# Four-layer block kernel: twenty turns written out in place of a loop of two, and a new order of the pieces on four engines

## Chip, cores and metric

The kernel runs on one core of a Trainium2 chip. The metric is the device time of one execution in microseconds (us), the median of several runs; less is better. The profile comes from one more execution.

## What is computed

Input x is 32 sequences of 256 tokens with 128 features, in fp32. Four layers follow one another, and each is `x = layernorm(x + layer(x))`, the norm over the features and without weights:

```python
q, k = rope(x @ Wq.T), rope(x @ Wk.T)         # 8 heads of 16
v, gate = x @ Wv.T, x @ Wg.T
num = (q @ (k.T @ v)) * scale + v.sum(tokens)
den = (q @ k.sum(tokens)) * scale + 256
layer1 = ((num / den + conv5(v)) * gate) @ Wo.T
layer2 = x @ W.T + lw[top1] * (x @ Wd[top1].T) @ Wu[top1].T   # ranks 1, 2, 4, 8
layer3 = softmax(mask(q @ k.T / sqrt(128))) @ v               # causal, one head
layer4 = sum(w[e] * swiglu_e(x) for 4 of 16 experts) + swiglu_shared(x)
```

In layer 2, `lw` is the softmax of four scaled cosine similarities and top1 its largest entry. In layer 4 a sigmoid router picks two of four groups of experts and then four experts; the sixteen experts have 64 hidden features each, the shared one 128.

## The kernel before, in words

**Blocks and turns.** The 8192 tokens are cut in 16 blocks of 512 (two sequences, four tiles of 128 tokens). A block goes through the kernel in five turns. Turn i works on layer 1 of block i (pieces whose names begin with `a_`), layer 2 and the projections of layer 3 of block i-1 (`b_`, `c_xT`, `c_project`, `c_value`), the attention of layer 3 and the router of block i-2 (`c_`, `r_`), the experts of block i-3 (`d_`), and the output of block i-4 (`d_yT`, `d_res`, `e_norm`). There are 20 turns. Turns 0 to 2 lack later layers, turns 16 to 19 earlier ones; turns 3 to 15 have all of `a`, `b`, `c` and `d`, and are called full here. The engines share no barrier: each runs its own list of pieces in order, and a piece begins with waits on semaphores that count what the others have finished. So the order of the pieces in the function `turn` of each engine sets the order of the work, and a piece whose input is late holds up all that stands behind it on its engine.

**Loop.** Each engine writes out turns 0 to 5 (`LEAD = 6`), then runs a hardware loop of two turns five times (turns 6 to 15), and then has turns 16 to 19 written out again. Two turns stand in a turn of the loop since some buffers alternate.

**Pieces on TensorE.** `a_xT_` transposes x (L378), `a_vT_` makes v transposed (L384), `a_qk` q and k (L390), `a_g_` the gate (L402), `a_v_` transposes the centred v back (L415), `a_kv` multiplies k and v (L406), `a_qT_` transposes q (L420), `a_num_` makes numerator and denominator (L424), `a_aT` transposes the result (L432), `a_out` applies Wo (L436). `b_small` (L449) makes all small projections of layer 2, `b_dnT` and `b_up` the low-rank part (L457, L461). `c_scores`, `c_pT`, `c_av` (L486, L500, L507) are layer 3's attention. `r_xT`, `r_gate` (L516, L520) feed the router, `d_cT` (L526) transposes the expert weights. The experts come in nine chunks of 128 hidden features, eight routed and one shared: `d_hidden(c)` (L532) writes gate and up products of chunk c into the banks GB and UB, in three products of split fp32r operands each, and `d_down(c)` (L548) adds the chunk's output in bank YB. d_hidden(c) waits for silu and for gu of chunk c-1, which empty GB and UB.

**ScalarE** evacuates most banks (`x0_hi`, `a_vT_`, `a_g_`, `a_v_`, `a_qT_`, `copy_xT`, `b_small`, `b_dnT`, `c_pT`, `c_qkv`, `r_hi`, `d_y`), takes exponentials (`c_exp`, `b_exp`, `r_exp`) and silu (`d_silu(c)`, L734), applies norms (`c_norm`, `b_layer_norm`, `e_norm`) and the first tap of the convolution (`a_tap0`, L676). Exponential and silu need different tables; a table load of 1.28 us stands before the first of either kind after the other.

**VectorE** multiplies silu by the up product (`d_gu(c)`, L1063) and that by the transposed expert weight (`d_hid(c)`, L1072), does rope (`a_rope`, L836), masks the k-v product into kv_m (`a_kv`, L845), adds the other four taps (`conv_tap`, L947), takes reciprocals of the denominator (`a_den`, L855), divides (`a_att`, L862), adds convolution and mean (`a_mix`), and takes row maxima (`c_max`), residual sums (`a_res`, `c_res`, `d_res`) and statistics of every norm (`norm_stats`, `b_res`, L1001). The router's small operations are `b_norm`, `b_logits`, `b_first`, `b_weigh` for layer 2 and `r_groups(0..4)`, `r_combine` for layer 4.

**GpSimd** subtracts the high parts (`x0_lo`, `x3_lo`), adds the two halves of rope (`a_rope`, semaphore g_qk), gates (`a_gate`) and turns statistics into scale and shift (`ln_of(k)`, one per norm). `split_late` splits the experts' weights into high and low parts once, in turn 1, on ScalarE (L629) and VectorE (L816). SP issues loads and stores (L309 on).

Of the kernel before, what the change touches and what calls it, by code (L numbers as in the profile page):

```python
# [111 lines left out]
def build(nc, x_dram, weight_dram, whole_dram, out_dram):  # L112
    blocks = x_dram.shape[0] // BLOCK
    LEAD = 6
    loops = (blocks - LEAD) // 2
    turns = blocks + 4
    assert blocks % 2 == 0 and loops > 0
# [8 lines left out]
    with ExitStack() as ctx:  # L126
# [183 lines left out]
        def _(sp):  # L310
# [24 lines left out]
            with sp.Fori(0, blocks // 2 - 3) as k:  # L335
                store(2 * k)
                load_after(2 * k + 4, 0)
                store(2 * k + 1)
                load_after(2 * k + 5, 1)
            for n in range(blocks - 6, blocks):  # L340
                store(n)
            sp.wait_ge(x_st.sem, x_st.at(blocks - 1))
# [3 lines left out]
        def _(pe):  # L346
# [73 lines left out]
            def a_qT_(n):  # L420
                pe.wait_ge(a_g.sem, a_g.at(n))
                transpose_tiles(A0, lambda t: qk[:, t, 0:P], ident).then_inc(p_qT.sem, 1)
# [139 lines left out]
            def turn(i, odd, load=None):  # L562
                a, b, c, d, e = live(i), live(i - 1), live(i - 2), live(i - 3), live(i - 4)
                if a: a_xT_(i, odd, load)
                if d: d_hidden(i - 3, 1 - odd, 0)
                if d: d_cT(i - 3)
                if c: c_scores(i - 2)
                if e: d_yT(i - 4)
# [3 lines left out]
                if a: a_qk(i)  # L572
                if c: c_av(i - 2)
                if b: b_xT(i - 1)
                if a: a_g_(i)
                if d: d_down(i - 3, 0)
                if b: b_small(i - 1)
                if a: a_v_(i)
                if d: d_hidden(i - 3, 1 - odd, 2)
                if a: a_kv(i)  # L580
                if a: a_qT_(i)
# [3 lines left out]
                if a: a_num_(i)  # L585
                if d: d_down(i - 3, 2)
                if c: r_xT(i - 2, odd)
                if d: d_down(i - 3, 3)
                if d: d_hidden(i - 3, 1 - odd, 5)
                if c: r_gate(i - 2)  # L590
                if b: b_dnT(i - 1)
                if d: d_down(i - 3, 4)
                if b: b_up(i - 1)
                if d: d_hidden(i - 3, 1 - odd, 6)
                if d: d_down(i - 3, 5)
                if a: a_aT(i)
                if d: d_hidden(i - 3, 1 - odd, 7)
                if d: d_down(i - 3, 6)
                if d: d_hidden(i - 3, 1 - odd, 8)
                if b: c_xT(i - 1)  # L600
                if a: a_out(i)
# [4 lines left out]

            for i in range(LEAD):
                turn(i, i % 2, i // 2)
            with pe.Fori(0, loops) as k:
                turn(2 * k + LEAD, 0, k + LEAD // 2)  # L610
                turn(2 * k + LEAD + 1, 1, k + LEAD // 2)
            for i in range(blocks, turns):
                turn(i, i % 2)
# [3 lines left out]
        def _(act):  # L617
# [126 lines left out]
            def turn(i, odd):  # L744
# [3 lines left out]
                if second(i): split_late()  # L748
                if c: c_exp(i - 2)
                if a: a_vT_(i)  # L750
                if c: c_pT(i - 2)
                if d: d_silu(i - 3, 1)
                if b: copy_xT(i - 1, 1, B0)
                if b: b_small(i - 1)
                if a: a_g_(i)
                if a: a_v_(i)
                if a: a_tap0(i)
                if d: d_silu(i - 3, 2)
                if a: a_qT_(i)
                if d: d_silu(i - 3, 3)  # L760
                if b: b_exp(i - 1)
                if c: c_norm(i - 2, odd)
                if d: d_silu(i - 3, 4)
                if c: r_hi(i - 2, odd)
                if d: d_silu(i - 3, 5)
                if c: r_exp(i - 2)
                if b: b_dnT(i - 1)
                if d: d_silu(i - 3, 6)
                if e: e_norm(i - 4)
                if d: d_silu(i - 3, 7)  # L770
# [6 lines left out]
            for i in range(LEAD):  # L777
                turn(i, i % 2)
            with act.Fori(0, loops) as k:
                turn(2 * k + LEAD, 0)  # L780
                turn(2 * k + LEAD + 1, 1)
            for i in range(blocks, turns):
                turn(i, i % 2)
# [3 lines left out]
        def _(dve):  # L787
# [298 lines left out]
            def turn(i, odd):  # L1086
                a, b, c, d, e = live(i), live(i - 1), live(i - 2), live(i - 3), live(i - 4)
                if d: d_gu(i - 3, 0)
                if c: c_max(i - 2)
                if d: d_hid(i - 3, 0)  # L1090
                if b: a_layer_norm(i - 1)
# [4 lines left out]
                if b: b_norm(i - 1, 0)  # L1096
                if d: d_hid(i - 3, 1)
                if d: d_gu(i - 3, 2)
                if b: b_norm(i - 1, 1)
                if d: d_hid(i - 3, 2)  # L1100
                if d: d_gu(i - 3, 3)
                if b: b_logits(i - 1)
                if a: a_kv(i)
                if d: d_hid(i - 3, 3)
# [3 lines left out]
                if d: d_gu(i - 3, 4)  # L1108
                if a: conv_tap(i, 2)
                if d: d_hid(i - 3, 4)  # L1110
                if a: conv_tap(i, 3)
                if a: conv_tap(i, 4)
                if d: d_gu(i - 3, 5)
                if a: a_den(i)
                if c: r_groups(i - 2, 0)
                if d: d_hid(i - 3, 5)
                if b: b_res(i - 1)
                if a: a_att(i)
                if c: r_groups(i - 2, 1)
                if d: d_gu(i - 3, 6)  # L1120
                if c: r_groups(i - 2, 2)
                if d: d_hid(i - 3, 6)
                if a: a_mix(i)
                if second(i): split_late()
                if c: r_groups(i - 2, 3)
                if d: d_gu(i - 3, 7)
# [3 lines left out]
                if a: a_res(i, odd)  # L1130
                if c: r_combine(i - 2)
                if b: c_value(i - 1)

            for i in range(LEAD):
                turn(i, i % 2)
            with dve.Fori(0, loops) as k:
                turn(2 * k + LEAD, 0)
                turn(2 * k + LEAD + 1, 1)
            for i in range(blocks, turns):
                turn(i, i % 2)  # L1140
# [3 lines left out]
        def _(pool):  # L1144
# [58 lines left out]
            def turn(i, odd):  # L1203
# [5 lines left out]
                if c: x3_lo(i - 2, odd)  # L1209
# [93 lines left out]
```

## Time and profile before

| | |
|---|---|
| median of 3 runs | 724.38 us (723.42 to 725.23) |
| span of the profiled execution | 722.4 us; the page gives no total beside it |
| instructions | 13085 |
| DMA | 12.51 MB, a mean of 17 GB/s |
| cores and dies | one core, mean granted clock 0.971 |

How to read it: the span goes from the first to the last instruction. PE is TensorE (matmuls), PEld its weight loads, DVE VectorE, ACT ScalarE, POOL GpSimd, SP SyncE. Matmuls overlap one another in the records, so the distance between their starts tells their cost better than their durations. An idle time is given with what ended it; "issue" means that the engine waited for nothing that the profile shows.

### The profile page before, as it was taken

How to read it: one execution, taken by the hardware profiler on the slowest of the kernel's cores; microseconds unless marked ns; L12 is line 12 of the kernel's file. 1: busy time of each engine (PE TensorE's matmuls, PEld its weight loads, DVE VectorE, ACT ScalarE, POOL GpSimd, SP SyncE). 2: the span in 40 equal slices, each digit the busy share in tenths (PEclk: the TensorE clock that was granted, in tenths of full speed). 3: DMA queues.
4: the chain of work that ended last, by engine and by line, in shares of the span. 5: the costliest groups of instructions: out<-in, count | busy, mean ns of one | idle time of the engine just before them, and what ended most of it. 6: DMA issues, size and time to landing. Idle time of an engine off the chain costs nothing.

```text
span 722.4 us, 13085 instructions
## 1 busy us (share of the span) xinstructions
PE 659.3 (91%) x3654; PEld 508.6 (70%) x3654; DVE 587.1 (81%) x1873; ACT 486.4 (67%) x978; POOL 309.0 (43%) x793
## 2 busy tenths in 40 slices
PE   3466679999999999999999999999999999999994
PEld 2354557787878777777878787777868787767652
DVE  1566778989898898889898898889897998877672
ACT  2243548587786878686877877686877868676623
POOL 1234443445453535536454535436454535340311
PEclk9787979999999999999999999999999999999997
DMA  6000000000000010101000000101000000000001
GB/s 226 12 4 15 1 16 0 16 1 16 15 15 15 1 30 2 31 0 29 0 15 16 5 25 0 30 0 29 0 21 9 15 0 0 15 1 15 16 0 30
DMA packets 18678, 12.51 MB, mean 17 GB/s; under 512 B 704, under 2 KB 18240, under 8 KB 18368
## 3 DMA queue, kind: packets, MB, share of 16 engines
q1 hardware_dynamic: 18624, 11.95, 5.5%
q8 instruction: 15, 0.25, 0.2%
q14 instruction: 39, 0.32, 0.1%
HBM read 7.75 MB, written 4.19 MB: 17 GB/s over the span
## 4 chain that ended last, share of the span: by engine, by line
PE 68%; DVE 14%; ACT 7%; issue 6%; POOL 3%; DMA 1%; DVEq 0%; ACTq 0%; SPq 0%; POOLq 0%
PE bank L556 13%; PE bank L351 8%; PE bank L353 8%; PE bank L352 8%; PE bank L360 8%; PE bank L439 2%; PE bank L466 2%; PE bank L411 2%; PE bank L454 2%; DVE conv L954 2%; DVE gu L1067 1%; PE bank L477 1%; PE bank L510 1%; PE bank L478 1%; PE bank L523 1%
## 5 line engine op out<-in xcount | busy, mean ns | idle before, releaser
L556 PE MATMUL bank<-hid,whole 128*128 128x512 f32 x288 | 147.2, 593 | 0.8 <-DVE hid L1070 0.8
L351 PE MATMUL bank<-x3T_hi,w_hi 128*128 128x512 f32 x288 | 138.2, 480 | 1.8 <-DVE gu L1067 1.4
L738 ACT ACTIVATE silu<-bank 128x512 f32<-128x512 f32 x144 | 86.4, 600 | 65.0 <-PE bank L353 61.9
L1067 DVE TENSOR_TENSOR gu<-silu,bank 128x512 f32<-128x512 f32 x128 | 86.7, 677 | 41.1 <-ACT silu L738 18.5
L353 PE MATMUL bank<-x3T_hi,w_lo 128*128 128x512 f32 x288 | 113.5, 394 | 0.0
L352 PE MATMUL bank<-x3T_lo,w_hi 128*128 128x512 f32 x288 | 112.7, 391 | 0.0
L1171 POOL TENSOR_TENSOR moment<-stats 128x4 f32<-128x4 f32 x192 | 44.8, 266 | 150.1 <-DVE stats L881 134.3
L1077 DVE TENSOR_TENSOR hid<-gu,bank 128x512 f32<-128x512 f32 x128 | 87.2, 681 | 1.8 <-PE bank L556 0.8
L351 PEld LDWEIGHTS bank<-x3T_hi,w_hi 128*128 128x128 f32 x288 | 54.2, 188 | 31.0 <-ACT silu L738 9.9
L1157 POOL TENSOR_TENSOR qk<-rope_c,rope_s 128x512 f32<-128x512 f32 x32 | 40.6, 1280 | 82.6 <-DVE rope_s L843 82.6
L1171 POOL TENSOR_TENSOR rstd<-moment,whole 128x4 f32<-128x4 f32 x64 | 64.7, 1011 | 5.0
L352 PEld LDWEIGHTS bank<-x3T_lo,w_hi 128*128 128x128 f32 x288 | 54.5, 189 | 16.3 <-issue 10.0
L353 PEld LDWEIGHTS bank<-x3T_hi,w_lo 128*128 128x128 f32 x288 | 54.0, 188 | 12.4
L556 PEld LDWEIGHTS bank<-hid,whole 128*128 128x128 f32 x288 | 49.7, 189 | 15.3 <-issue 7.2
L1201 POOL TENSOR_TENSOR x3T_lo<-x3T,x3T_hi 128x512 fp32r<-128x512 f32 x16 | 22.0, 1375 | 87.9 <-ACT x3T_hi L728 87.9
L738 ACT ACT_TABLE_LOAD x45 | 57.7, 1283 | 0.8
L954 DVE SCALAR_TENSOR_TENSOR conv<-vT,whole,conv 128x512 f32<-128x512 f32 x64 | 54.4, 850 | 0.8
L881 DVE BATCH_NORM_STATS2 stats<-res 128x6 f32<-128x128 f32 x192 | 41.9, 281 | 1.6
L1171 POOL TENSOR_TENSOR moment<-moment,whole 128x4 f32<-128x4 f32 x192 | 35.6, 202 | 5.0
L644 ACT ACTIVATE x<-bank,shift,rstd 128x128 f32<-128x128 f32 x64 | 24.1, 457 | 19.1 <-POOL shift L1171 19.1
L360 PEld LDWEIGHTS bank<-whole,x 128*128 128x128 f32 x192 | 23.7, 144 | 18.3 <-ACT x L644 7.9
L360 PE MATMUL bank<-whole,x 128*128 128x128 f32 x192 | 30.0, 280 | 7.1 <-ACT x L644 6.8
(196 smaller groups left out, 1635.7 us busy)
## 6 DMA issues: line engine op xcount, KB each, us to landing
x_in<-x SPq DMA_DIRECT2D x16, 256.0 KB, 2.9
out<-x SPq DMA_DIRECT2D x16, 256.0 KB, 2.3
whole<-w_whole SPq DMA_DIRECT2D x1, 1198.5 KB, 5.7
w_raw<-w SPq DMA_DIRECT2D x1, 1152.0 KB
w_raw<-w SPq DMA_DIRECT2D x1, 546.0 KB, 7.0
whole<-w_whole SPq DMA_DIRECT2D x16, 32.0 KB
whole<-w_whole SPq DMA_DIRECT2D x1, 64.0 KB
```

Of the source, the lines that this page charges most:

```text
L351: mm(out, wh, mh, start=True, stop=False)
L352: mm(out, wh, ml, start=False, stop=False)
L353: return mm(out, wl, mh, start=False, stop=True)
L360: last = nc.tensor.transpose(out[0:parts, t * P:(t + 1) * P], src(t), eye)
L556: mm(YB[:], whole[:, a:a + P], hid[:, c % 2], start=c == 0, stop=c == CHUNKS).then_inc(p_w2.sem, 1)
L738: fn(silu[:, c % 2], GB[:], ACT.Silu).then_inc(a_silu.sem, 1)
L881: nc.vector.bn_stats(stats[k][:, t, :], res[k][:, t, :]).then_inc(v_st[k].sem, 1)
L954: stt(conv[:], vT[:, :, j:j + SEQ], taps[:, j:j + 1], conv[:], ALU.mult, ALU.add).then_inc(v_conv.sem, 1)
L1067: tt(gu[:, c % 2], silu[:, c % 2], UB[:], ALU.mult).then_inc(v_gu.sem, 1)
L1077: tt(hid[:, c % 2], gu[:, c % 2], CB[:], ALU.mult).then_inc(v_hid.sem, 1)
L1157: tt(qk[:, 2 * h:2 * h + 2, :].rearrange("p t d -> p (t d)"), rope_c[:, h], rope_s[:, h], ALU.add).then_inc(g_qk.sem, 1)
L1171: tt(out, in0, in1, op).then_inc(g_ln[k].sem, 1)
```

## The change

All engines: the loop goes, and all 20 turns are written out. SP's loop goes as well. In the order of the pieces:

- TensorE: in the first part of the turn d_yT, c_scores, d_cT in place of d_cT, c_scores, d_yT; b_xT before c_av; d_hidden 2 before a_v_; a_qT_ behind d_down 2 and before r_xT, a_kv behind r_xT (it stood before a_qT_); a_num_ behind b_up; a_aT behind d_hidden 7; a_out before c_xT; d_down 3 to 5 one or two pieces later.
- a_qT_ waits for g_qk as well. a_kv, which now stands behind it, has waited for g_qk before.
- ScalarE: x1T's copy before silu 1; the gate before b_small; silu 2 before tap 0; split_late behind tap 0; c_norm and silu 4 before a_v_ and b_exp; a_qT_ behind b_dnT; silu 7 before e_norm.
- VectorE: a_layer_norm before hid 0; a_kv between taps 2 and 3; r_groups 0 to 3 in one run between taps 3 and 4; b_res before a_den, gu 6 between a_den and a_att; split_late behind a_res.
- GpSimd: x3_lo behind a_gate.

```diff
             for n in range(4):
                 load_after(n, n % 2)
-            with sp.Fori(0, blocks // 2 - 3) as k:
-                store(2 * k)
-                load_after(2 * k + 4, 0)
-                store(2 * k + 1)
-                load_after(2 * k + 5, 1)
-            for n in range(blocks - 6, blocks):
+            for n in range(blocks):
                 store(n)
+                if n + 6 < blocks:
+                    load_after(n + 4, n % 2)
...
             def a_qT_(n):
                 pe.wait_ge(a_g.sem, a_g.at(n))
+                pe.wait_ge(g_qk.sem, g_qk.at(n))
...
+                if e: d_yT(i - 4)
+                if c: c_scores(i - 2)
                 if d: d_cT(i - 3)
-                if c: c_scores(i - 2)
-                if e: d_yT(i - 4)
                 if a: a_vT_(i)
                 if d: d_hidden(i - 3, 1 - odd, 1)
                 if c: c_pT(i - 2)
                 if a: a_qk(i)
+                if b: b_xT(i - 1)
                 if c: c_av(i - 2)
-                if b: b_xT(i - 1)
                 if a: a_g_(i)
                 if d: d_down(i - 3, 0)
                 if b: b_small(i - 1)
+                if d: d_hidden(i - 3, 1 - odd, 2)
                 if a: a_v_(i)
-                if d: d_hidden(i - 3, 1 - odd, 2)
-                if a: a_kv(i)
-                if a: a_qT_(i)
                 if d: d_hidden(i - 3, 1 - odd, 3)
                 if d: d_down(i - 3, 1)
                 if d: d_hidden(i - 3, 1 - odd, 4)
-                if a: a_num_(i)
                 if d: d_down(i - 3, 2)
+                if a: a_qT_(i)
                 if c: r_xT(i - 2, odd)
-                if d: d_down(i - 3, 3)
+                if a: a_kv(i)
                 if d: d_hidden(i - 3, 1 - odd, 5)
                 if c: r_gate(i - 2)
                 if b: b_dnT(i - 1)
+                if d: d_down(i - 3, 3)
+                if d: d_hidden(i - 3, 1 - odd, 6)
+                if b: b_up(i - 1)
+                if a: a_num_(i)
                 if d: d_down(i - 3, 4)
-                if b: b_up(i - 1)
-                if d: d_hidden(i - 3, 1 - odd, 6)
+                if d: d_hidden(i - 3, 1 - odd, 7)
+                if a: a_aT(i)
                 if d: d_down(i - 3, 5)
-                if a: a_aT(i)
-                if d: d_hidden(i - 3, 1 - odd, 7)
                 if d: d_down(i - 3, 6)
                 if d: d_hidden(i - 3, 1 - odd, 8)
+                if a: a_out(i)
                 if b: c_xT(i - 1)
-                if a: a_out(i)
...
-            for i in range(LEAD):
+            for i in range(turns):
                 turn(i, i % 2, i // 2)
-            with pe.Fori(0, loops) as k:
-                turn(2 * k + LEAD, 0, k + LEAD // 2)
-                turn(2 * k + LEAD + 1, 1, k + LEAD // 2)
-            for i in range(blocks, turns):
-                turn(i, i % 2)
...
                 if d: d_silu(i - 3, 0)
                 if a: x0_hi(i)
-                if second(i): split_late()
                 if c: c_exp(i - 2)
                 if a: a_vT_(i)
                 if c: c_pT(i - 2)
+                if b: copy_xT(i - 1, 1, B0)
                 if d: d_silu(i - 3, 1)
-                if b: copy_xT(i - 1, 1, B0)
+                if a: a_g_(i)
                 if b: b_small(i - 1)
-                if a: a_g_(i)
-                if a: a_v_(i)
+                if d: d_silu(i - 3, 2)
                 if a: a_tap0(i)
-                if d: d_silu(i - 3, 2)
-                if a: a_qT_(i)
+                if second(i): split_late()
                 if d: d_silu(i - 3, 3)
-                if b: b_exp(i - 1)
                 if c: c_norm(i - 2, odd)
                 if d: d_silu(i - 3, 4)
+                if a: a_v_(i)
+                if b: b_exp(i - 1)
                 if c: r_hi(i - 2, odd)
                 if d: d_silu(i - 3, 5)
                 if c: r_exp(i - 2)
                 if b: b_dnT(i - 1)
+                if a: a_qT_(i)
                 if d: d_silu(i - 3, 6)
+                if d: d_silu(i - 3, 7)
                 if e: e_norm(i - 4)
-                if d: d_silu(i - 3, 7)
...
                 if c: c_max(i - 2)
+                if b: a_layer_norm(i - 1)
                 if d: d_hid(i - 3, 0)
-                if b: a_layer_norm(i - 1)
                 if e: d_res(i - 4, odd)
...
                 if d: d_hid(i - 3, 4)
                 if b: b_first(i - 1)
                 if b: b_weigh(i - 1)
                 if a: conv_tap(i, 1)
-                if d: d_gu(i - 3, 4)
                 if a: conv_tap(i, 2)
-                if d: d_hid(i - 3, 4)
+                if d: d_gu(i - 3, 5)
+                if a: a_kv(i)
                 if a: conv_tap(i, 3)
+                if c: r_groups(i - 2, 0)
+                if c: r_groups(i - 2, 1)
+                if c: r_groups(i - 2, 2)
+                if c: r_groups(i - 2, 3)
                 if a: conv_tap(i, 4)
-                if d: d_gu(i - 3, 5)
-                if a: a_den(i)
-                if c: r_groups(i - 2, 0)
                 if d: d_hid(i - 3, 5)
                 if b: b_res(i - 1)
+                if a: a_den(i)
+                if d: d_gu(i - 3, 6)
                 if a: a_att(i)
-                if c: r_groups(i - 2, 1)
-                if d: d_gu(i - 3, 6)
-                if c: r_groups(i - 2, 2)
                 if d: d_hid(i - 3, 6)
+                if d: d_gu(i - 3, 7)
                 if a: a_mix(i)
-                if second(i): split_late()
-                if c: r_groups(i - 2, 3)
-                if d: d_gu(i - 3, 7)
                 if d: d_hid(i - 3, 7)
                 if c: r_groups(i - 2, 4)
                 if d: d_gu(i - 3, 8)
                 if a: a_res(i, odd)
+                if second(i): split_late()
...
                 if b: b_norm(i - 1)
-                if c: x3_lo(i - 2, odd)
                 if e: ln_of(3, i - 4)
                 if b: ln_of(1, i - 1)
                 if a: a_gate(i)
+                if c: x3_lo(i - 2, odd)
                 if a: ln_of(0, i)
```

The loops of ScalarE, VectorE and GpSimd go as TensorE's does.

## Rows read from the trace of the kernel before

**Rows 1.** The page, parts 1 and 2: busy times, and the span in 40 slices.

```profile
PE 659.3 (91%) x3654; PEld 508.6 (70%) x3654; DVE 587.1 (81%) x1873; ACT 486.4 (67%) x978; POOL 309.0 (43%) x793
...
PE   3466679999999999999999999999999999999994
...
PEclk9787979999999999999999999999999999999997
```

**Rows 2.** Busy times by stretch, cut at turn starts: length, then busy (count) per engine, granted clock.

```profile
11.10:33.03 21.93, 12.03 (x58) 9.78 (x59) 8.12 (x18) 5.53 (x13) 5.05 (x4) 0.90 0.13 30
33.03:67.51 34.48, 20.17 (x103) 15.86 (x103) 21.08 (x59) 12.71 (x28) 13.79 (x36) 0.72 0.06 16
67.51:102.65 35.14, 23.56 (x150) 19.28 (x149) 24.52 (x88) 16.12 (x43) 15.03 (x36) 0.85 0.03 8
...
182.46:222.29 39.83, 39.83 (x231) 31.23 (x229) 35.94 (x117) 30.48 (x61) 19.47 (x50) 1.00 0.05 14
...
262.06:301.88 39.82, 39.82 (x231) 31.22 (x230) 36.01 (x117) 30.55 (x61) 19.48 (x50) 1.00 0.05 15
301.88:342.46 40.58, 40.02 (x230) 31.25 (x229) 35.77 (x117) 30.54 (x61) 19.38 (x50) 1.00 0.05 14
...
382.26:422.76 40.50, 40.03 (x231) 31.25 (x230) 35.75 (x117) 30.55 (x61) 19.38 (x50) 1.00 0.05 14
...
462.56:503.30 40.74, 40.06 (x230) 31.22 (x229) 35.74 (x117) 30.55 (x61) 19.36 (x50) 1.00 0.05 14
...
543.08:583.58 40.50, 40.01 (x231) 31.23 (x230) 35.75 (x117) 30.54 (x61) 19.37 (x50) 1.00 0.03 7
...
623.30:658.47 35.17, 33.98 (x173) 23.59 (x172) 27.78 (x97) 25.64 (x48) 11.47 (x36) 1.00 0.03 8
658.47:688.22 29.75, 26.93 (x129) 19.05 (x128) 19.95 (x57) 17.69 (x34) 6.80 (x23) 1.00 0.03 10
688.22:712.41 24.19, 22.53 (x82) 14.02 (x81) 15.57 (x33) 8.12 (x15) 2.78 (x11) 1.00 0.04 12
```

**Rows 3.** Timeline at the first jump, turn 8: start, us, engine, instruction, idle time before.

```profile
305.62 0.69 DVE L1067 TENSOR_TENSOR gu<-silu,bank 128x512 f32<-128x512 f32 x1 [1.85 <-issue]
...
311.31 0.49 PE L510 MATMUL bank<-cv,probT 128*128 128x128 f32 x2 [0.56 <-ACT probT L709]
```

**Rows 4.** Timeline of turn 7, ScalarE and VectorE around silu 2.

```profile
276.38 0.82 ACT L677 ACTIVATE conv<-vT,whole 128x512 f32<-128x512 f32 x1
...
277.73 0.69 DVE L1067 TENSOR_TENSOR gu<-silu,bank 128x512 f32<-128x512 f32 x1 [1.25 <-ACT silu L738]
```

**Rows 5.** VectorE in turn 7: the taps by tile, then the timeline den and b_res.

```profile
L954 DVE SCALAR_TENSOR_TENSOR conv<-vT,whole,conv x4: 744/748/1169, 283.9 to 287.8; 128x512 f32<-128x512 f32 x4
...
289.11 0.25 DVE L858 TENSOR_SCALAR den<-bank 128x16 f32<-128x16 f32 x2
...
290.29 0.88 DVE L1004 BATCH_NORM_STATS2 stats<-bank 128x6 f32<-128x128 f32 x4
```

**Rows 6.** Timeline of VectorE in turn 0, taps and den.

```profile
23.67 3.10 DVE L954 SCALAR_TENSOR_TENSOR conv<-vT,whole,conv 128x512 f32<-128x512 f32 x4
...
26.69 0.25 DVE L858 TENSOR_SCALAR den<-bank 128x16 f32<-128x16 f32 x2
```

**Rows 7.** Timeline of turn 1: split_late on ScalarE, a part of it on VectorE.

```profile
35.10 1.06 ACT L633 ACTIVATE w_hi<-w_raw 128x1024 fp32r<-128x1024 f32 x1
...
59.45 2.28 DVE L821 TENSOR_TENSOR w_lo<-w_raw,w_hi 128x1024 fp32r<-128x1024 f32 x1
```

**Rows 8.** Timeline of turn 2: GpSimd's last step for norm 2, ScalarE's norm, VectorE's b_res.

```profile
81.38 0.20 POOL L1171 TENSOR_TENSOR shift<-mean,rstd 128x4 f32<-128x4 f32 x1
...
83.32 1.63 ACT L714 ACTIVATE x<-res,shift,rstd 128x128 f32<-128x128 f32 x4
...
90.96 0.89 DVE L1004 BATCH_NORM_STATS2 stats<-bank 128x6 f32<-128x128 f32 x4 [0.84 <-PE bank L467]
```

**Rows 9.** Timeline of TensorE at the end of turn 17 and in turn 18.

```profile
691.15 0.66 PE L360 MATMUL bank<-whole,comb 128*128 128x128 f32 x4 [0.97 <-DVE comb L1060]
```

More of the change, by code:

```diff
@@ L113, in build @@
     blocks = x_dram.shape[0] // BLOCK
-    LEAD = 6
-    loops = (blocks - LEAD) // 2
     turns = blocks + 4
-    assert blocks % 2 == 0 and loops > 0
+    assert blocks % 2 == 0
     def live(n):
@@ L775, in turn @@
                 if d: d_y(i - 3)
[L777 to L782, printed above, removed]
+            for i in range(turns):
                 turn(i, i % 2)
@@ L1095, in turn @@
                 if d: d_gu(i - 3, 1)
-                if b: b_norm(i - 1, 0)
                 if d: d_hid(i - 3, 1)
                 if d: d_gu(i - 3, 2)
+                if b: b_norm(i - 1, 0)
                 if b: b_norm(i - 1, 1)
@@ L1101, in turn @@
                 if d: d_gu(i - 3, 3)
+                if d: d_hid(i - 3, 3)
                 if b: b_logits(i - 1)
-                if a: a_kv(i)
-                if d: d_hid(i - 3, 3)
+                if d: d_gu(i - 3, 4)
+                if d: d_hid(i - 3, 4)
                 if b: b_first(i - 1)
@@ L1130, in turn @@
                 if a: a_res(i, odd)
+                if second(i): split_late()
                 if c: r_combine(i - 2)
                 if b: c_value(i - 1)
[L1134 to L1139, printed above, removed]
+            for i in range(turns):
                 turn(i, i % 2)
@@ L1212, in turn @@
                 if a: a_gate(i)
+                if c: x3_lo(i - 2, odd)
                 if a: ln_of(0, i)
-            for i in range(LEAD):
-                turn(i, i % 2)
-            with pool.Fori(0, loops) as k:
-                turn(2 * k + LEAD, 0)
-                turn(2 * k + LEAD + 1, 1)
-            for i in range(blocks, turns):
+            for i in range(turns):
                 turn(i, i % 2)
```

## The prediction

> **What bounds it now.** I read the page's busy times first. TensorE is busy 91% of the span, VectorE 81%, and the slices show TensorE at nine tenths or more from about 110 us on, with low digits only in the fill, where the granted clock is also below 1 [rows 1]. So I cut the trace at the starts of the turns (the transposes of x_in on TensorE) and asked for the busy times turn by turn [rows 2]. Three regimes come out. In the full turns 3 to 15 TensorE is busy for the whole turn, 39.8 us each, VectorE for some 36 us and ScalarE for 30.5. A different order cannot shorten such a turn by more than a tenth or so, but it can lengthen it. The second regime is turns 8, 10, 12 and 14, each the first after the loop has jumped back: 40.58, 40.50, 40.74 and 40.50 us. The third is fill and drain: turns 0 to 2 take 21.9, 34.5 and 35.1 us for 12.0, 20.2 and 23.6 us of TensorE work, and turns 16 to 18 hold 5.7 us in which TensorE is idle. There waits decide, and an order can win.
>
> The times below are set against the profiled execution: its span is 722.4 us. The page gives no more of it than that; the median of the runs, 724.4, lies 2.0 above, which I take as what lies around the span and leave alone. What a measurement of this kernel can tell from no change is about 0.3%, 2.2 us.
>
> **The loop written out.** At the jump VectorE has had all its inputs for 1.85 us and does not issue: the row names "issue" and no engine. The delay passes through the softmax to TensorE, which waits 0.56 us for probT before it multiplies by the values [rows 3]. Against the 39.8 us of their neighbours the four turns lose 0.78 + 0.70 + 0.94 + 0.70 = 3.1 us [rows 2]. No turn has a jump afterwards: **-3.1**. From below, nothing is gained if straight code is fetched as slowly as the jump's target; against it, turns 0 to 5 and 16 to 19 are straight code already, and turn 5 takes 39.83 us [rows 2]. From above, 3.1 is all that there is. SP's queue issues the same loads and stores in the same sequence (4 loads, then store n, load n+4), so nothing moves on it.
>
> The Trainium skill (Runtime: NRT & Kernel Launch, Instruction fetch mechanics) says that prefetch is sequential and that a taken branch outside the window stalls for a fetch; the trace agrees. The same section speaks of blocks of 256 instructions whose refill is "mostly hidden": by it the written-out code costs about nothing.
>
> **Full turns, order of TensorE.** I laid the pieces end to end with the intervals of a full turn (hidden 1.4 to 1.5 us, down 0.86, scores 1.8, qk 1.5, project 1.7, the rest 0.4 to 1.4) and checked each wait, times from the turn's start.
> - yT, scores, cT in place of cT, scores, yT: the scores start as before; comb is ready long before. Nothing. hid 0 on VectorE now follows the layer norm, 1.0 us later, and still precedes down 0 by 4 us.
> - b_xT before c_av: both wait for probT; the product with the values ends 0.35 us later, just as VectorE gets to it. At most 0.1.
> - ScalarE takes x1T ahead of silu 1, and with it silu 1's table load; silu 1 ends near 11.9 in place of 10.5, its reader on VectorE starts at 12.8. Nothing. silu 2 now precedes tap 0: in the trace VectorE waits 1.25 us for exactly this silu, behind the 0.82 us tap [rows 4]. VectorE gains about 0.9 us.
> - qT now waits for the second half of qk from GpSimd. It stands at 19.3 us; GpSimd's two adds end near 12. The added wait, and what is queued behind it on TensorE (r_xT, kv, hidden 5), costs nothing in a full turn.
> - kv, then num, stand later: num moves from 19.8 to 27.5 us, behind up. kv_m and qT are ready by 26.2. But den, then att, now follow num within 0.3 us, and VectorE has gu 6 behind den: den can start at 28.7, and two den, one reciprocal and gu 6 end near 30.0 where hidden 7 wants its bank at 29.95; att then ends at 30.7 where aT stands at 30.7. Before, both den and gu 6 had their inputs long before they started; den opens this stretch [rows 5]. I charge **0.1 to 0.2 us a turn** here.
> - x3_lo goes behind a_gate on GpSimd and ends near 35.4; its reader is hidden 0 of the next turn at 40.2, and ln_of(0) behind it has no input before 37. Nothing. With it gone from there, a convolution tap that took 1.17 us beside it goes back to 0.75 [rows 5].
> - r_groups 1 to 3 are now one chain with gaps, 0.25 us more on VectorE ahead of gu 6, paid by the gain at silu 2. c_xT, project and out keep their slack to within 0.1.
>
> Two transpose blocks (qT, r_xT) now stand back to back; I expect under 0.1 us a turn from that. Thirteen turns at 0.1 net: **+1.3**. The bounds are -1 (no stall, a little from the blocks) and +5.2 (0.4 a turn, if den, gu 6 and att are late by VectorE's 0.3).
>
> The trace shows a tap at 1.17 us beside GpSimd's add and 0.74 alone. The Trainium skill (GPSIMD Engine Reference, Specifications) says that GpSimd shares its SBUF interfaces with VectorE's instructions of two SBUF inputs; the trace agrees. By this rule x3_lo's new place, beside small router operations, costs VectorE less than its old one, beside the taps.
>
> **Turn 0.** Four taps now run 3.1 us ahead of den, which starts at 26.69 though num was issued at 24.4 [rows 6]. With two taps ahead of kv_m, in time in which VectorE was idle, den starts when num lands, near 25.5: **-1.2**. tap 0 before v_one costs kv about 0.2, inside this.
>
> **Turn 1.** split_late leaves an idle stretch of ScalarE (35.1 us on) and stands before a_v_: two activations like the 1.06 us each and two an eighth as wide [rows 7], some 2.4 us in all. It delays v_one from 46.1 to about 48.8 and kv with it; the router's small chain on VectorE ends near 51 either way, and num now follows up. att comes near 56.5, 0.4 later than now. Given back: on VectorE split_late goes behind a_res. It no longer runs beside GpSimd's layer norm and a_gate, where one part took 2.28 us [rows 7], so oT and out come 1 us sooner; the 2.8 us then stand ahead of c_value, which needs project and value first. Net **-0.2**, between -1.5 and +2.5 (all of ScalarE's delay).
>
> **Turn 2.** c_norm stands ahead of b_exp, whose logits wait for GpSimd; now it starts at 83.3 though its scale is there at 81.6 [rows 8]. r_xT, gate, dnT and up come 1.5 us sooner, kv later. VectorE is the one that ends it: taps, kv_m, the router, then b_res about 0.9 earlier than 90.96 [rows 8]. **-0.9**, between -1.7 and +1.
>
> **Drain.** In turn 17 TensorE waits for the last hid and then, in turn 18, for comb, 0.97 us [rows 9]. r_exp gets its input 0.5 us sooner because hidden 5 and gate precede down 3, and silu 7 no longer waits behind e_norm (1.65 us); gu 8, the combine and cT come some 0.8 earlier. In turn 18 yT goes into the wait for comb: 0.4. **-1.2**, from 0 to -2.
>
> **Sum.** -3.1 + 1.3 - 1.2 - 0.2 - 0.9 - 1.2 = -5.3: a span of 717.1 us, a median of 719.1, 0.7% less.
>
> **Rivals.**
> 1. The full turns run clean, fill and drain give all they can: -3.1 from the jumps, -1.0 from the full turns, -4.0 from fill and drain = -8.1, 716.3. For it: every wait but one has slack by the rows. Against: three places stand within 0.1 us. Chance 0.18.
> 2. The attention's tail becomes a wait (slower). In each full turn num, den, gu 6, hidden 7, att, aT form one chain with no slack. If b_res and hid 5 on VectorE are late, den starts late and TensorE idles twice, for gu 6 and for att. If den stands behind a whole b_res after num has landed, that is 0.88 us a turn [rows 5]; thirteen turns cost 11.4 in place of 1.3: 729.2. It overtakes everything else from (5.3 + 1.3)/13 = 0.5 us a turn; half of it, 0.4 to 0.5, leaves 723.0 to 724.3, no change. For it: VectorE is busy 36 of 39.8. Against: it loses its 1.25 us wait ahead of this. Chance 0.08 for slower, 0.09 for the half.
> 3. Written-out code is fetched late on some engine: the loop's 3.1 us do not come back, 722.2. Against: the straight turns. Chance 0.05.
> 4. The clock. Turns 1 and 2 were granted 0.72 and 0.85 of full speed in the mean [rows 2], that is stretches at 1.2 GHz in place of 2.4, and TensorE had idled before them. Other gaps can move these stretches by 1 or 2 us either way; this widens the forecast and is no case of its own.
>
> **Numbers.** Forecast 0.60, for 717 to 721.5. The range 714.5 to 723.5 takes in rivals 1 and 3 and half of the second. Faster by over 0.3% (under 722.2): 0.60 + 0.18 + half of rival 3's 0.05, some 0.81. Within: the half of rival 2 and the rest of 3, 0.11. Slower: 0.08.
>
> **What would show it.** Right: turns cut as above are 39.7 to 40.0 us throughout, with none at 40.5; no VectorE wait by "issue" at a turn's start; den in turn 0 near 25.5; gu 2 waits under 0.5 us for silu. Wrong: a wait of TensorE for gu or att before hidden 7 or aT of 0.4 us or more in every full turn; full turns above 40.2; turn 1 longer than 35.5 us; a granted clock under 1 after turn 2.

## The result, and the profile after

The changed kernel takes 727.83 us (median of 4 runs, 727.12 to 728.54) against 724.48 for the kernel before, measured beside it: a ratio of 1.0044, 95% interval 1.0031 to 1.0058. It is slower by 0.4%, where the forecast was 0.7% faster. The profiled execution took 727.15 us, its span 725.3.

The page of the changed kernel, parts 1 and 2, against [rows 1]:

```profile
PE 669.0 (92%) x3654; PEld 516.6 (71%) x3654; DVE 608.3 (84%) x1873; ACT 484.5 (67%) x978; POOL 295.4 (41%) x793
...
PE   3567679999999999999999999999999999999994
...
PEclk9756859999999999999999999999999999999998
```

TensorE runs the same 3654 instructions and is busy for 9.7 us longer. The third, fourth and sixth slice of the clock's row say why: 5, 6 and 5 tenths where [rows 1] have 8, 7 and 7 (the fifth slice is 8 against 9). The same cut at the turns' starts as in [rows 2]: length, busy time and count of each engine, and the granted clock as the third number from the end.

```profile
10.79:32.22 21.43, 13.16 (x59) 10.49 (x60) 8.12 (x18) 5.31 (x13) 5.05 (x4) 0.89 0.13 36
32.22:71.23 39.01, 25.73 (x104) 20.96 (x103) 20.38 (x59) 12.70 (x28) 15.93 (x36) 0.59 0.05 14
71.23:109.54 38.31, 27.13 (x149) 23.38 (x149) 26.04 (x93) 16.09 (x42) 15.22 (x38) 0.73 0.03 8
...
189.19:229.00 39.81, 39.81 (x230) 31.08 (x229) 37.44 (x117) 30.42 (x61) 18.25 (x51) 1.00 0.05 15
268.84:308.68 39.84, 39.84 (x231) 31.07 (x230) 37.43 (x117) 30.42 (x61) 18.23 (x51) 1.00 0.05 14
308.68:348.51 39.83, 39.83 (x230) 31.05 (x229) 37.42 (x117) 30.41 (x61) 18.23 (x51) 1.00 0.05 14
```

Against [rows 2], turn 0 is 0.5 us shorter, turn 1 4.5 longer and turn 2 3.2 longer. The rest is shorter, by 3.0 and 1.0 us: turn 3 starts at 109.54 (102.65 before) and turn 15 at 587.47 (583.58), so these twelve turns take 477.9 us for 480.9, and from the start of turn 15 to the end of the span it is 137.8 us for 138.8. With 0.3 from the start of turn 0 this makes -0.3 - 0.5 + 4.5 + 3.2 - 3.0 - 1.0 = +2.9, the difference of the spans. The whole loss stands in turns 1 and 2, and there the busy time of TensorE, for one matmul more and one less, grew by 5.6 and 3.6 us. The time in which TensorE is idle even fell, from 14.3 to 13.3 us and from 11.6 to 11.2: it does not wait more, it works longer at 1.2 GHz.

The timeline of TensorE in the changed kernel shows both the gaps and the slow work behind them, first in turn 1, then in turn 2:

```profile
49.48 2.15 PE L406 MATMUL bank<-v_one,qk 128*128 128x136 f32 x8 [3.11 <-ACT v_one L645]
51.43 1.06 PE L355 MATMUL bank<-whole,down_x 128*96 128x128 f32 x4
...
55.79 2.12 PE L425 MATMUL bank<-kv_m,qT 128*128 128x136 f32 x8
59.36 0.66 PE L355 MATMUL bank<-whole,att 128*128 128x128 f32 x4 [1.45 <-DVE att L852]
62.33 2.08 PE L435 MATMUL bank<-whole,oT 128*128 128x128 f32 x8 [2.31 <-POOL oT L1144]
...
87.37 1.12 PE L355 MATMUL bank<-whole,x 128*128 128x128 f32 x4 [4.77 <-ACT x L705]
88.28 2.02 PE L406 MATMUL bank<-v_one,qk 128*128 128x136 f32 x8
90.09 1.73 PE L519 MATMUL bank<-w_raw,x3T 128*128 128x16 f32 x8
```

In turn 1 split_late on ScalarE delays v_one, and kv waits 3.11 us; in turn 2 the router's transposes wait 4.77 us for ScalarE's norm and keep kv behind them. Before, TensorE's idle time here was cut into pieces with work between them: kv waited about 1 us, num 0.9 us in turn 1 and 2.2 in turn 2. Now more of it stands in one piece, and the work of kv, dnT, up, num and out that follows runs at half rate: kv takes 2.15 us where at the full clock, in turn 1 of the kernel before, it takes 1.17:

```profile
46.82 1.17 PE L411 MATMUL bank<-v_one,qk 128*128 128x136 f32 x8 [1.05 <-ACT v_one L654]
```

How the clock goes in the two kernels, in stretches of 3 us. Changed kernel:

```profile
27.00:30.00 3.00, 0.89 (x4) 0.49 (x4) 0.97 (x3) 0.00 (x0) 0.97 (x1) 0.57 0.00 0
...
39.00:42.00 3.00, 3.00 (x14) 2.81 (x13) 0.83 (x3) 1.92 (x7) 0.00 (x0) 0.50 0.02 5
42.00:45.00 3.00, 3.00 (x16) 2.68 (x15) 1.95 (x5) 0.93 (x3) 2.25 (x2) 0.58 0.01 3
45.00:48.00 3.00, 1.38 (x13) 1.14 (x12) 1.06 (x4) 2.77 (x6) 1.16 (x2) 0.98 0.00 0
48.00:51.00 3.00, 1.51 (x7) 1.55 (x8) 2.39 (x16) 1.45 (x4) 0.17 (x1) 0.50 0.00 0
51.00:54.00 3.00, 2.32 (x11) 1.84 (x11) 2.93 (x6) 1.08 (x2) 0.00 (x0) 0.50 0.00 0
...
84.00:87.00 3.00, 0.00 (x0) 0.00 (x0) 0.34 (x2) 1.33 (x4) 2.37 (x4) 0.74 0.00 0
87.00:90.00 3.00, 2.63 (x12) 2.63 (x13) 2.60 (x15) 1.99 (x5) 0.00 (x0) 0.50 0.00 0
```

Kernel before, the same part of turn 1 (0.8 us later in its own time) and of turn 2:

```profile
45.00:48.00 3.00, 1.95 (x17) 1.74 (x17) 1.25 (x4) 2.02 (x4) 1.91 (x2) 1.00 0.00 0
48.00:51.00 3.00, 1.59 (x12) 1.18 (x10) 2.46 (x16) 0.70 (x2) 0.20 (x1) 1.00 0.00 0
51.00:54.00 3.00, 2.12 (x16) 1.80 (x16) 2.89 (x5) 0.59 (x1) 0.00 (x0) 1.00 0.00 0
...
84.00:87.00 3.00, 1.65 (x14) 1.21 (x12) 2.76 (x13) 2.03 (x5) 0.08 (x1) 1.00 0.00 0
87.00:90.00 3.00, 2.32 (x21) 2.07 (x21) 2.93 (x6) 0.82 (x2) 1.19 (x1) 1.00 0.00 0
```

In the changed kernel the clock comes back at about 45 us and is at 0.50 again from 48, behind the gap before kv. Before, it holds from 45 to 54, and falls behind the next gap, ahead of att's transposes.

### The profile page after: what moved, and what is told of

Its sections match the earlier page's. It is cut to its first block, busy times and chain, and to the rows that moved or that the text cites. A ratio compares the mean times of both kernels' runs of the same rounds, so it can differ in the third digit from the quotient of the medians.

```text
span 725.3 us, 11732 instructions
## 1 busy us (share of the span) xinstructions
PE 669.0 (92%) x3654; PEld 516.6 (71%) x3654; DVE 608.3 (84%) x1873; ACT 484.5 (67%) x978; POOL 295.4 (41%) x793
## 4 chain that ended last, share of the span: by engine, by line
PE 87%; DVE 4%; POOL 3%; ACT 3%; issue 1%; DMA 1%; SPq 0%; DVEq 0%; ACTq 0%; POOLq 0%
PE bank L552 16%; PE bank L346 11%; PE bank L355 10%; PE bank L348 10%; PE bank L347 10%; PE bank L462 3%; PE bank L435 2%; PE bank L406 2%; PE bank L473 2%; PE bank L479 2%; PE bank L425 2%; PE bank L474 2%; PE bank L519 2%; PE bank L450 2%; PE bank L500 1%
## 5 line engine op out<-in xcount | busy, mean ns | idle before, releaser
L346 PE MATMUL bank<-x3T_hi,w_hi 128*128 128x512 f32 x288 | 147.7, 513 | 1.9 <-DVE gu L1053 1.7
L552 PE MATMUL bank<-hid,whole 128*128 128x512 f32 x288 | 145.0, 594 | 0.1
L1152 POOL TENSOR_TENSOR moment<-stats 128x4 f32<-128x4 f32 x192 | 35.5, 218 | 261.1 <-DVE stats L990 135.1
L346 PEld LDWEIGHTS bank<-x3T_hi,w_hi 128*128 128x128 f32 x288 | 54.3, 189 | 36.4 <-issue 15.3
L940 DVE SCALAR_TENSOR_TENSOR conv<-vT,whole,conv 128x512 f32<-128x512 f32 x64 | 47.8, 746 | 2.4 <-ACT conv L668 1.8
L1152 POOL TENSOR_TENSOR moment<-moment,whole 128x4 f32<-128x4 f32 x192 | 35.1, 199 | 5.0
L827 DVE TENSOR_TENSOR rope_c<-bank,whole 128x512 f32<-128x512 f32 x32 | 22.0, 686 | 14.3 <-PE bank L394 12.6
L1177 POOL TENSOR_TENSOR x0T_lo<-x0T,x0T_hi 128x512 fp32r<-128x512 f32 x16 | 20.3, 1267 | 28.1 <-ACT x0T L641 28.1
```

The costliest lines, as they stand in the source:

```text
L346: mm(out, wh, mh, start=True, stop=False)
L552: mm(YB[:], whole[:, a:a + P], hid[:, c % 2], start=c == 0, stop=c == CHUNKS).then_inc(p_w2.sem, 1)
L940: stt(conv[:], vT[:, :, j:j + SEQ], taps[:, j:j + 1], conv[:], ALU.mult, ALU.add).then_inc(v_conv.sem, 1)
L1152: tt(out, in0, in1, op).then_inc(g_ln[k].sem, 1)
```

## The experiments

All times are medians; "fill" is the time from the start of turn 0 to that of turn 3 in the profiled execution, 91.6 us before and 98.8 after. Theory A: the new order makes longer chains of waits in turns 1 and 2. Theory B: the chains are about as long, and the time goes through the stretches at 1.2 GHz. In the first, third, fifth to seventh and ninth kernel, a second function `turn_old` holds the old order of each engine.

**1. Old order in turns 0 to 2.** `(turn_old if i in (0, 1, 2) else turn)(i, i % 2)` on all four engines.

> The changed kernel with the old order of the pieces on all four engines in turns 0 to 2, and the new order from turn 3 on. Theory A (the loss sits in the order of turns 1 and 2 alone; the written-out code and the drain gain about 4): turns 0 to 2 take 22, 34.5 and 35.1 us again, and the time is 724.5 - 3 - 1 = 720.5. Rival (the long way of the fill comes from the written-out code or from the split of fetches, not from the order): the fill stays near 99 us long and the time near 727.5.

Measured 721.23 us (ratio 0.9942, 0.9926 to 0.9959). Turns 0 to 2 take 22.4, 33.8 and 36.6 us, the rest stays as in the changed kernel (478.1 and 137.9 us). The loss lies in the order of the fill. That does not tell A from B.

**2. split_late alone in its old places.**

```diff
                 if a: x0_hi(i)
+                if second(i): split_late()
...
                 if a: a_tap0(i)
-                if second(i): split_late()
```

and on VectorE behind a_mix in place of behind a_res.

> The changed kernel with split_late alone back in its old places (ScalarE: behind x0_hi; VectorE: behind a_mix). Theory A, first half: the 3.1 us wait of kv for v_one in turn 1 goes, turn 1 falls from 39.0 to some 35 us and turn 2 stays near 38, so about 724. If the clock's low stretches shift with it, turn 2 may move by 1 or 2 us as well. Rival (split_late only fills time that other waits would hold): turn 1 stays above 38 and the time near 727.5.

Measured 727.76 us (1.0049, 1.0026 to 1.0072), turn 1 38.25 us: a miss. The wait ahead of kv fell from 3.11 to 0.55 us, and TensorE then waited 2.57 us for dnT; dnT, up, num and out of turn 1 still ran at half rate, while kv, ahead of the gap, took 1.17 us. The idle time had moved, not gone:

```profile
49.64 1.09 PE L355 MATMUL bank<-whole,down_x 128*96 128x128 f32 x4 [2.57 <-DVE down_x L931]
```

Turn 2, in which nothing was changed, took 39.97 us in this execution, against 38.31.

**3. Written out, old order in all turns** (`turn_old` for every i, with the added wait).

> The old order everywhere, all turns written out (and the one added wait). Theory A: the four turns at 40.5 to 40.7 us fall to 39.8 and nothing else moves: 724.5 - 3.1 = 721.4. Rival (written-out code is fetched late somewhere): 724 or more. The distance from this run to the one with the old fill alone tells what the new order gives in full turns and drain: 1 us by theory A.

Measured 722.27 us (0.9952, 0.9936 to 0.9969). Turns 3 to 15 are 39.8 us each. This is the loop's part alone, and it lies 1.0 us above the first kernel, which is what the new order gives in full turns and drain. Its fill, with the order of the kernel before, took 94.2 us (23.4, 34.2 and 36.6) in the profiled execution, against 91.6 and, in the first experiment, 92.8. So the lengths of single turns of the fill, each read from one execution, differ by about 1 us and more for the same order; the medians, and differences well beyond that, are what the argument can rest on.

**4. Unread matmuls in the gaps of the fill.** The changed kernel, with matmuls of 512 columns into a bank that is free in turns 0 to 2; nobody reads them.

```diff
+            def warm(count):
+                for _ in range(count):
+                    mm(GB[:], ident, const("cos"), start=True, stop=True)
...
+                warm({2: 5}.get(i, 0))
                 if c: r_xT(i - 2, odd)
+                warm({1: 3, 2: 0}.get(i, 0))
                 if a: a_kv(i)
```

and 4 before vT in turn 1, 1 before aT and 2 before out in turns 0 to 2.

> The changed kernel with matmuls that nobody reads (bank GB, which turns 0 to 2 do not use) in TensorE's idle stretches of turns 0 to 2: 4 before vT and 3 before kv in turn 1, 5 before r_xT in turn 2, 1 before aT and 2 before out in each. They cost at most some 0.9 us each where the stretch is shorter than they are. Theory B (most of the loss is the granted clock, which falls after TensorE idles and then makes kv, up, num, out, project and value take twice as long): the clock stays at full speed through turns 1 and 2, both get 2 to 4 us shorter, and the time is 721 to 724. Rival (the waits themselves are the loss, the clock a bystander): no gain, 727 to 730.

Measured **712.49 us** (0.9829, 0.9813 to 0.9846), the fastest of all kernels here, and far below the 721 to 724 expected of theory B. The three turns:

```profile
10.96:30.75 19.79, 13.71 (x64) 9.84 (x65) 8.13 (x18) 5.42 (x13) 5.05 (x4) 1.00 0.15 35
30.75:61.20 30.45, 24.63 (x125) 15.56 (x124) 19.83 (x59) 12.71 (x28) 13.68 (x29) 1.00 0.07 18
61.20:94.64 33.44, 27.62 (x166) 19.98 (x165) 25.37 (x91) 16.09 (x42) 16.37 (x44) 1.00 0.03 9
```

TensorE has 21 matmuls more to do (two records each), no piece of work and no wait was taken away, and the fill is 15.1 us shorter. Its num in turn 1, in the timeline of this kernel, beside the 55.79 us row above:

```profile
50.23 1.14 PE L425 MATMUL bank<-kv_m,qT 128*128 128x136 f32 x8
```

**5 and 6. Old order in turn 1 alone, in turn 2 alone.**

> The changed kernel with the old order of all four engines in turn 1 alone. If each turn's loss is its own (the gap ahead of kv in turn 1, the gap ahead of r_xT in turn 2), turn 1 falls from 39.0 to about 34.3 us and turn 2 stays at 38.3: 723.3 us. If turn 2's stretches at 1.2 GHz are handed on from turn 1, turn 2 falls as well, to 36 or less, and the time is 721 or less. If only the order at the turns' seams matters, nothing changes: 727.8.

> The changed kernel with the old order of all four engines in turn 2 alone. If each turn's loss is its own: turn 1 stays at 39.0 us, turn 2 falls from 38.3 to about 35.5, 725 us. If turn 2's loss is handed on from turn 1, turn 2 stays near 38: 727.5.

Measured 721.32 us (0.9962, 0.9947 to 0.9977) and 726.01 (1.0014, 1.0004 to 1.0024). Turns 1 and 2 in the two kernels:

```profile
31.37:64.46 33.09, 19.09 (x104) 15.43 (x103) 20.90 (x59) 12.71 (x28) 12.65 (x32) 0.75 0.05 15
64.46:102.49 38.03, 26.85 (x151) 23.10 (x149) 26.05 (x93) 16.12 (x42) 16.82 (x43) 0.73 0.03 9
```

```profile
31.41:69.86 38.45, 24.71 (x103) 19.86 (x103) 20.39 (x59) 12.71 (x28) 15.96 (x36) 0.68 0.05 14
69.86:108.90 39.04, 27.47 (x149) 22.25 (x149) 25.23 (x92) 15.95 (x41) 15.14 (x38) 0.73 0.03 8
```

Turn 1's order carries most: 5.9 us on turn 1. With turn 2's old order behind a new turn 1, turn 2 is 39.04 us, no shorter than with the new one; if turn 2's loss were its own, it would have been 35.5. The same order took 35.1 us in the kernel before and 36.6 behind an old turn 1 in the first experiment. A turn's length goes with its clock, and its clock isn't a matter of its own order alone: with the new order and no matmuls added to it, turn 2 took from 37.3 us at a clock of 0.82 (experiment 8) to 40.4 us at 0.67 (experiment 10).

**7 and 9. Old order in turns 0 to 2 with unread matmuls** in the gaps that this order has: 4 before vT in turn 1, kv 1, num 1 or 2, gate 1, aT 1 or 2, c_xT 3, out 2 in turn 0; the ninth has 6 before vT, 1 before dnT, and one more before aT and out in turn 0 and before aT in turn 2.

> The old order in turns 0 to 2 (as in the first experiment, 721.2 us) with matmuls that nobody reads put ahead of the pieces for which TensorE waits: before vT 4, kv 1, num 1, aT 2, c_xT 3 in turn 1; kv 1, num 2, gate 1, aT 1, c_xT 3 in turn 2; aT 2 and out 2 in turn 0. Theory clock (the order costs through the stretches at 1.2 GHz and nearly nothing beside them): the fill comes down to that of the new order with such matmuls, within 1 us, so 712 to 713.5 us. Theory order (the new order has longer chains of waits in turns 1 and 2 whatever the clock): the old fill stays ahead by the 6.6 us that lie between the two now, about 706.

> The seventh kernel (old order in turns 0 to 2, unread matmuls in the gaps) with more of them, so that no stretch of the fill is left at 1.2 GHz. Theory clock: at the full clock the new order of the fill is the shorter one, by the 1.2 us of turn 0 and little beside them, so this kernel stays behind the changed kernel with such matmuls (712.5 us): 713 to 714 us, from the start of turn 0 to that of turn 3 some 85.2 us against 83.7. Theory order: the old order is ahead once the last low stretches are gone, 711 us or less.

Measured 714.28 us (0.9856, 0.9832 to 0.9880) and 714.09 (0.9847, 0.9828 to 0.9865). The seventh still had 0.95 in turns 1 and 2, the ninth has no stretch below 1:

```profile
10.89:31.99 21.10, 16.67 (x71) 11.46 (x72) 8.11 (x18) 5.42 (x13) 5.05 (x4) 1.00 0.13 36
31.99:62.45 30.46, 27.60 (x132) 16.86 (x131) 20.91 (x59) 12.72 (x28) 12.57 (x32) 1.00 0.06 17
62.45:96.53 34.08, 29.68 (x170) 20.51 (x169) 23.89 (x86) 16.12 (x42) 15.49 (x39) 1.00 0.03 9
```

This is the run that decides between the theories. At the full clock the two orders stand 21.10 to 19.79, 30.46 to 30.45 and 34.08 to 33.44: the new order of the fill is 2.0 us *shorter*. Of this the 1.3 us of turn 0 stand in the seventh kernel too (21.04 us). The 0.6 of turn 2 are less sure: the ninth has ten unread matmuls there, where the fourth and the seventh have eight, and the seventh took 33.63 us although its clock was lower. Without the matmuls the new order is 6.6 us longer (727.8 against 721.2). The low clock costs the old order 7.1 us (721.2 - 714.1) and the new one 15.3 (727.8 - 712.5). Both figures are lower bounds, since the added matmuls can themselves delay the pieces behind them. Theory A is out. The medians, 712.5 and 714.1, stand 1.6 us apart, with the new order ahead.

By the clocks of its turns, the changed kernel's fill is at 1.2 GHz for some 57 us. TensorE is busy for 66.0 of the fill's 98.8 us; taken in proportion, an estimate, that is 38 of the 57, and half of it, 19 us, is what the low clock adds to the work. The runs give at least 15.3; where the rest goes is not taken apart. The Trainium skill (TensorE: Matmul & The Clock Gate, Terms) puts the penalty at all the time spent at the low clock, times one less the ratio of the clocks. An estimate by that rule is 29 us; the runs do not agree with it.

**8. The matmuls in turns 0 and 1 alone.**

> The changed kernel with unread matmuls in turns 0 and 1 alone (4 before vT, 3 before kv, 1 before aT and 2 before out in turn 1; 1 before aT and 2 before out in turn 0), none in turn 2. If the gap ahead of r_xT brings turn 2 its own low clock, turn 1 is 30.5 us and turn 2 stays near 38: about 717 us. If turn 2's low clock is handed on from turn 1, turn 2 is near 34 and the time about 713.

Measured 716.69 us (0.9894, 0.9860 to 0.9929); turn 1 30.46 us, turn 2 37.26 at a clock of 0.82. So turn 2 has a low clock of its own, and left alone it costs 3.8 us against the fourth kernel. It comes in two stretches, one behind the gap ahead of r_xT (4.76 us) and a longer one behind the gaps ahead of aT and out (1.45 and 2.35 us), which the fourth kernel also filled:

```profile
78.00:81.00 3.00, 3.00 (x16) 3.00 (x15) 2.66 (x13) 1.39 (x4) 0.00 (x0) 0.50 0.00 0
81.00:84.00 3.00, 2.32 (x19) 2.06 (x20) 2.93 (x10) 1.30 (x3) 0.00 (x0) 0.97 0.00 0
...
90.00:93.00 3.00, 2.86 (x12) 2.46 (x12) 2.83 (x7) 0.31 (x2) 1.10 (x1) 0.50 0.00 0
```

**10 and 11. One gap filled:** `warm(3)` before kv in turn 1, or `warm(5)` before r_xT in turn 2.

> The changed kernel with three unread matmuls ahead of kv in turn 1 and nothing else. If each idle gap of TensorE brings on the low stretch that follows it, the one from about 48.6 to 59 us goes and turn 1 falls from 39.0 to about 36.5 us: 725 us. If the low clock of turn 1 comes from how the turn begins (it starts at 1.2 GHz), nothing changes: 727.8.

> The changed kernel with five unread matmuls ahead of the transposes of x for the router in turn 2 (the wait of 4.77 us) and nothing else. If this gap brings on the low stretch from 86 to 106 us, turn 2 falls from 38.3 to about 34.5 us and turn 1 stays at 39: 724 us. If the low clock comes of the whole thin fill, turn 2 stays over 37: 727.

Measured 724.43 us (722.85 to 726.79 over 10 runs; 0.9988, 0.9974 to 1.0003) and 725.09 (720.77 to 726.01; 0.9983, 0.9965 to 1.0001). Turns 1 and 2 of the tenth, then turn 2 of the eleventh and two stretches of it:

```profile
31.62:66.62 35.00, 23.61 (x109) 17.27 (x109) 20.09 (x59) 12.70 (x28) 15.92 (x36) 0.74 0.06 16
66.62:107.03 40.41, 29.23 (x151) 24.60 (x150) 26.73 (x94) 16.70 (x42) 15.48 (x38) 0.67 0.03 7
```

```profile
70.00:107.52 37.52, 30.53 (x160) 23.41 (x160) 26.55 (x94) 16.70 (x42) 15.49 (x38) 0.82 0.03 8
...
87.00:90.00 3.00, 2.31 (x19) 1.85 (x17) 2.84 (x11) 1.60 (x5) 0.00 (x0) 1.00 0.00 0
90.00:93.00 3.00, 2.92 (x16) 2.92 (x17) 2.93 (x11) 0.51 (x2) 0.00 (x0) 0.63 0.00 0
```

Three unread matmuls ahead of kv (two records each) shorten turn 1 by 4.0 us, more than the 2.5 expected (by 3.4 against the 38.4 that turn 1 took in the sixth and eleventh kernels); and turn 2, in which nothing changed, grows by 2.1. In the eleventh the clock holds through the filled gap, to 90, then falls with TensorE nearly always busy; turn 2 gains 0.8 us of the 3.8 expected. So single gaps give back part, and what they give is partly taken elsewhere; only the fill without any long gap ran at 1.00 throughout.

**12. num early.** The second kernel, and in turn 1 num before dnT on TensorE, qT's copy before b_exp on ScalarE and den before b_res on VectorE.

> The second kernel (split_late back in its old places on ScalarE and VectorE, 727.8 us, turn 1 38.25 us) with num in its old place in turn 1 as well: ahead of dnT and up on TensorE, with qT's copy on ScalarE and den on VectorE moved to match. If num's place behind dnT and up makes turn 1 long, turn 1 falls to about 34.3 us: 723.8 us. If it is another move (the four taps, out ahead of c_xT), turn 1 stays above 37: 727.

Measured 730.71 us (1.0071, 1.0047 to 1.0095), turn 1 41.5 us: a miss on the other side. Now num waits for kv_m, which VectorE does behind the layer 2 router and two taps, and dnT and up wait behind num:

```profile
51.72 2.15 PE L425 MATMUL bank<-kv_m,qT 128*128 128x136 f32 x8 [4.46 <-DVE kv_m L838]
```

One piece put back on its own makes a gap of 4.46 us, longer than the 2.57 ahead of dnT in the second kernel. What num's place behind up costs is not shown by this run, since kv_m stayed behind two taps; moved without kv_m, num gains nothing.

## Why the prediction was wrong, and where it was right

**The step that failed** is the fourth rival: "Other gaps can move these stretches by 1 or 2 us either way; this widens the forecast and is no case of its own." The low clock costs the new order about 8 us more than the old one (15.3 - 7.1). The rows for it had been read: clocks of 0.72 and 0.85, TensorE idle before the falls [rows 2]. What was missing was to ask, for each move in turns 1 and 2, how long a gap of TensorE it makes, and to price the work behind it at both rates. The gaps were even named: "It delays v_one from 46.1 to about 48.8 and kv with it", which came true (kv at 49.48), and r_xT ahead of kv. They were costed as waits that other work would hide; att was to come 0.4 us later in turn 1, and its transposes came 4.0 later (27.1 us after the turn's start in place of 23.1), since kv, dnT, up and num ran at half rate ahead of it.

Point by point, with what the runs give beside each term:

| term | forecast | measured | from |
|---|---|---|---|
| loop written out | -3.1 | -3.3 | experiment 3, turns 3 to 14, 477.6 us against 480.9 |
| order in full turns | +1.3 | +0.3 | 477.9 against 477.6 |
| turn 0 | -1.2 | -0.5; at the full clock -1.3 | experiments 4 and 9 |
| turn 1 | -0.2 | +4.5; at the full clock 0.0 | the same |
| turn 2 | -0.9 | +3.2; at the full clock -0.6 at most | the same |
| drain | -1.2 | -1.0 | span less the start of turn 15 |

The working of the waits held: the three terms of the fill add up to -2.3 in the forecast and, between two kernels at the full clock, to something from -1.3 to -2.0. Turn 0 came as forecast even with the clock left alone: the profiled execution of the changed kernel has it 0.5 us shorter, but the six other kernels that have the same turn 0 (2, 5, 6, 10, 11 and 12) took 20.65 to 20.67 us, 1.3 us less than the kernel before. In turn 0 den starts at 25.66 (forecast 25.5); all full turns are 39.8 us; there is no VectorE wait by "issue" left at a turn's start; gu 2 no longer waits for silu. The waits of VectorE in turn 7 of the changed kernel, against the 1.25 us of [rows 4]:

```profile
DVE gu L1053 <- PE bank L348: 0.4, 1, 0.4
DVE neg_max L996 <- PE bank L494: 0.3, 1, 0.3
DVE hid L1063 <- PE bank L552: 0.2, 1, 0.2
```

TensorE waits for nothing in that turn, so rival 2, the tail of the attention, did not come. "Turn 1 longer than 35.5 us" stood in the list of what would show the forecast wrong, and it is what did.

A second, smaller error is the sentence that x3_lo's new place "costs VectorE less than its old one". The taps are all at 746 ns now, where one had lost 0.42 us, but two small router operations now meet GpSimd's work: gscore meets the end of its gating (0.88 us for 0.17) and g_diff meets x3_lo and pays 1.03 us (changed kernel, turn 7):

```profile
301.68 0.88 DVE L969 TENSOR_TENSOR gscore<-cross,inner 128x16 f32<-128x16 f32 x1
302.49 1.28 POOL L1182 TENSOR_TENSOR x3T_lo<-x3T,x3T_hi 128x512 fp32r<-128x512 f32 x1
302.60 1.25 DVE L971 TENSOR_TENSOR g_diff<-gscore 128x64 f32<-128x64 f32 x1
```

g_diff takes 0.22 us in the kernel before. VectorE is busy 37.4 us of a full turn in place of 36.0; its slack covers that, and the time does not show it.

## What to carry to other kernels

Where TensorE is idle in parts, price a new order twice: the waits, and the rate at which the work behind each gap runs. Two orders with the same total of idle time differ when one gathers it ahead of a chain of matmuls; here that cost about 8 us, against a gain in waits of 2.0 at most. Before arranging such a stretch by its waits, fill its gaps with matmuls that nobody reads: that took 15.3 us from this kernel and 7.1 from the old order, and only then does the better order show.

## What the runs showed of the hardware that was not expected

- In turns 1 and 2 the granted clock was 0.58 to 0.85 wherever the gaps of the turn were left as they were, and 1.00 where all of them were filled. It stayed at 0.50 through stretches in which TensorE was always busy (39 to 42 us above), and in the eleventh kernel it fell while TensorE was busy for 2.92 of 3 us. Which gap brings on which fall is left open: in the tenth kernel a filled gap in turn 1 went with a lower clock in turn 2 (0.67 against 0.73).
- Executions of one program differ with the clock that they are granted. In the eleventh kernel (720.8 to 726.0 us over 10 runs) the two fastest runs, 720.8 and 721.3 us, had a mean clock of 0.973 and the other eight 0.964 to 0.970; in the tenth the fastest (722.9) had 0.970 and the slowest (726.8) 0.959. With the whole fill at the full clock the runs lie within 1.4 us (712.4 to 713.8, four runs, and 714.0 to 715.3, four runs), with the clock left alone or single gaps filled within 1.4 to 5.2. That the low stretches fall elsewhere from run to run would explain it; only one execution of each was profiled, so this is not shown.
- A VectorE operation of 64 columns and 0.22 us takes 1.25 us when it starts 0.11 us behind a GpSimd operation of 1.28 us: it ends 0.08 us after it. gscore, which began while GpSimd's gating ran, ended 0.03 us after that. So in both rows what the meeting costs is what was left of GpSimd's operation, and a small operation can lose more than a tap did. The Trainium skill (SBUF — State Buffer, SBUF: two separate sides) calls the port pair that the two share an exclusive lock, held for the whole instruction by whichever of them starts first, for VectorE operations with two SBUF inputs as these are. The trace agrees in these two rows.
- The eight more turns that now stand in the code (20 in place of 12) cost nothing that the trace shows: 39.8 us in every turn, with no "issue" wait of VectorE at a turn's start, where each jump had cost 0.7 to 0.9 us [rows 2].
